# Experts in three fp32r products of split operands, their weights split during attention

## The reference

```
x = x + xattn(layernorm(x), ctx)      # fp8 quantise/dequantise both, one product per batch
hidden = layernorm(x)                 # B=4, S=512, D=512
q, k, v = rmsnorm(hidden) @ w.T       # 16 query heads, 4 key/value heads, hd=128
attn = causal softmax attention with rope and q/k norms
hidden = hidden + attn @ o_w.T
h2 = rmsnorm(hidden) * ffn_norm_w
topv, topi = top_k(softmax(h2 @ gate_w.T), 2)     # E = 8 experts, I = 352
eg, eu = h2 @ wg[e].T, h2 @ wu[e].T
moe = sum over the 2 experts of topw * (silu(eg) * eu) @ wd[e].T
x = x + hidden + moe
```

## Time and profile before

| | |
|---|---|
| time, median of 3 runs | 1544.74 us (1543.94 to 1544.88) |
| the profiled execution | 1543.88 us; its span 1542.1 us |
| PE busy | 1332.3 us, 86% |
| DVE / ACT / POOL busy | 786.9 / 639.6 / 377.8 us |
| PE: up products of the experts (L1515) | 197.2 us |
| PE: down products of the experts (L1532) | 107.0 us |
| mixer, dispatch, experts by their first instructions | 0, 1167.3, 1190 us |

### The profile page before, as it was taken

How to read it: one execution, slowest core, us unless ns; L and a number is a source line. 1 busy time by engine, 2 the same in 40 slices (tenths; PEclk the granted TensorE clock), 3 DMA queues, 4 the chain that set the end, 5 groups by cost and what they waited for, 6 DMA issues and landing times. The chain is left out here.

```text
span 1542.1 us, 20420 instructions
## 1 busy us (share of the span) xinstructions
PE 1332.3 (86%) x6416; PEld 971.2 (63%) x6416; DVE 786.9 (51%) x2389; ACT 639.6 (41%) x2114; POOL 377.8 (25%) x545
## 2 busy tenths in 40 slices
PE   2876989799799989989998999999892799999996
PEld 1564757677576767777676777777671455555653
DVE  7667756556675554577555454544525122222221
ACT  6446644455564545466454544544530111111111
POOL 0322211222222122132212223223101123332331
PEclk9897999999899999999999999999995899999998
DMA  2260324413333241223214122320218833333332
GB/s 89 90 238 21 124 81 166 157 64 129 143 83 121 70 164 56 109 83 83 109 55 161 50 91 82 104 116 4 79 55 270 315 65 69 62 62 69 66 59 40
DMA packets 44505, 156.38 MB, mean 101 GB/s; under 512 B 7089, under 2 KB 7985, under 8 KB 35185
## 3 DMA queue, kind: packets, MB, share of 16 engines
q1 hardware_dynamic: 30624, 129.89, 22.7%
q0 software_dynamic: 10848, 24.71, 9.0%
q10 hardware_dynamic: 2928, 0.49, 0.2%
HBM read 111.00 MB, written 44.06 MB: 101 GB/s over the span
## 5 line engine op out<-in xcount | busy, mean ns | idle before, releaser
L1151 DVE TENSOR_SCALAR_CACHE_REDUCE prob<-bank,nscale 128x128 f32<-128x128 f32 (+3 forms) x256 | 135.3, 546 | 281.7 <-PE bank L614 280.4
L434 POOL TENSOR_TENSOR prob<-prob,rtotal 128x128 f32<-128x128 f32 (+2 forms) x192 | 118.5, 623 | 431.3 <-DVE rtotal L1157 404.7
L846 ACT ACTIVATE pT<-bank 128x512 f32<-128x512 f32 (+3 forms) x256 | 104.1, 432 | 263.3 <-PE bank L622 263.0
L840 ACT ACTIVATE prob<-prob,bias 128x128 f32<-128x128 f32 (+3 forms) x256 | 144.9, 566 | 163.2 <-DVE prob L1151 161.8
L1515 PE MATMUL gu<-we,xT 128*128 x624 | 197.2, 470 | 2.3 <-DVE xT L1578 1.4
L578 PE MATMUL bank<-w_hi,hT_hi 128*128 128x512 f32 x480 | 177.1, 369 | 3.4 <-DVE rot L1116 3.4
L633 PE MATMUL bank<-pT,v 128*128 128x512 f32 (+3 forms) x512 | 176.8, 447 | 2.1 <-ACT pT L846 1.5
L578 PE MATMUL bank<-w_hi,hT_lo 128*128 128x512 f32 x480 | 165.2, 344 | 0.0
L578 PE MATMUL bank<-w_lo,hT_hi 128*128 128x512 f32 x480 | 165.1, 344 | 0.0
L411 POOL TENSOR_TENSOR r<-r,rot 128x640 f32<-128x640 f32 x60 | 96.3, 1604 | 280.1 <-DVE rot L1116 280.1
L1515 PEld LDWEIGHTS gu<-we,xT 128*128 128x128 f32 x624 | 116.6, 192 | 65.7 <-issue 5.0
(11 more groups left out here) (274 smaller groups left out, 2548.3 us busy)
## 6 DMA issues: line engine op xcount, KB each, us to landing
w_hi<-ws_scratch SPq DMA_DIRECT2D x24, 1024.0 KB, 5.0
w_lo<-ws_scratch SPq DMA_DIRECT2D x24, 1024.0 KB, 7.3
we<-in_wexp SPq DMA_DIRECT2D x8, 2176.0 KB, 22.4
stage<-in_wqkvo SPq DMA_DIRECT2D x40, 256.0 KB, 3.0
ws_scratch<-w_hi SPq DMA_DIRECT2D x7, 1024.0 KB, 3.9
ws_scratch<-w_lo SPq DMA_DIRECT2D x7, 1024.0 KB, 7.1
w_hi<-ws_scratch SPq DMA_DIRECT2D x12, 512.0 KB, 5.9
w_lo<-ws_scratch SPq DMA_DIRECT2D x12, 512.0 KB, 6.8
```

Of the source, the lines that this page charges most:

```text
L434: nc.gpsimd.tensor_tensor(p, p, rtotal[:, 4 * h + q:4 * h + q + 1].broadcast_to([P, KEYS[q]]), ALU.mult).then_inc(prob_ready, 1)
L840: nc.scalar.activation(p, p, ACT.Exp, bias=bias[:, 4 * h + q:4 * h + q + 1], scale=-1.0, accum_out=total[:, 4 * h + q:4 * h + q + 1]).then ...
L846: nc.scalar.activation(pT[:, PT_AT[j]:PT_AT[j] + QS[j]], bank[PT + j % 2][:, 0:QS[j]], ACT.Copy).then_inc(pt_copied, 1)
L1151: nc.vector.tensor_scalar(prob[(G * it + h) % (LAG + 1)][:, P_AT[q]:P_AT[q] + KEYS[q]], bank[SC + q % 2][:, 0:KEYS[q]], nscale[it % 2][:, ...
```

## The change

The weights of the experts are split in the mixer. From iteration 5 on, 10 of the 12 places of an iteration get a unit `ew`, 96 in all (12 pieces for each expert: 8 of 352 columns, 4 of 384). A unit is one ACT instruction (hi, scaled by `ffn_norm_w` where it is a gate or up weight), one DVE instruction (lo, written over the raw piece), and on SP one load and two saves. The split weights go to `wx_scratch` in DRAM, 4.4 MB for each expert. In SP's queue the instructions of an iteration are spread over its places in order to stand beside the pieces.

```
@@ mixer: where the units stand, and what they do
+SPLIT_E = [(0, 2), (0, 3), (1, 1), (1, 2), (1, 3), (2, 1), (2, 2), (2, 3), (3, 1), (3, 2)]
+FIRST_E = 5
+    if it >= FIRST_E and slot in SPLIT_E:            # at the end of units()
+        m = (it - FIRST_E) * len(SPLIT_E) + SPLIT_E.index(slot)
+        if m < NPIECE:
+            yield "ew", m
+            def hi_exp(m):                            # ACT
+                act.wait_ge(stage_in[n % RING_W], 16 * (n // RING_W + 1))
+                if m >= RING_E:                       # RING_E = 2
+                    act.wait_ge(ehi_saved[m % RING_E], 16 * (m // RING_E))
+                nc.scalar.activation(o, i, ACT.Copy, scale=wcolf[:, k:k + 1]).then_inc(exp_hi, 1)
+            def lo_exp(m):                            # DVE
+                dve.wait_ge(exp_hi, m + 1)
+                nc.vector.scalar_tensor_tensor(o, i, wcolf[:, k:k + 1], hi, ALU.mult, ALU.subtract).then_inc(exp_lo, 1)
@@ mixer, SP
-                if HKV <= it + 2 < NIT:
-                    load_q(it + 2)
-                    load_kv(it + 2)
+                for h in range(G):
+                    for place in range(1, 4):
+                        for kind, m in units(it, h, place):
+                            if kind == "ew":
+                                save_exp(m)           # waits exp_hi, saves hi; waits exp_lo, saves lo
+                                if m + RING_W < NPIECE:
+                                    load_exp(m + RING_W)   # waits until lo of m is saved
...
+                        if (h, place) == (2, 1) and HKV <= it + 2 < NIT:
+                            load_q(it + 2)
+                        if (h, place) == (2, 2) and HKV <= it + 2 < NIT:
+                            load_kv(it + 2)
@@ mixer, POOL
-            add_hidden(B - 1)
@@ dispatch
-                sp.dma_start(we[:, e * ECOLS:(e + 1) * ECOLS], wexp[e]).then_inc(w_in[e], 16)     # e = 1 to 7
+            load_expert(sp, 0, False)
+            load_expert(sp, 0, True)                  # expert 0 alone, 4 DMAs
+            pool.wait_ge(sources, 1)                  # POOL, when idg is ready
+            for i in range(NG):
+                pool.indirect_dma_start(xg[i][:, :], None, row_dram, ...).then_inc(x_in[i], 16)
+            nc.scalar.activation(iotas[:, :, :], iotab.unsqueeze(2).broadcast_to([P, P, JT]), ACT.Copy).then_inc(spread, 1)
-                pe.wait_ge(onehots, n + 1)
-                last = nc.tensor.matmul(rps[:, :], oh[:, n, :], rhs[:, :, :, n], ...)
+                pe.wait_ge(onehots, 1 if n < NT else 2)
+                last = nc.tensor.matmul(rps[:, :], oh[:, :, n], rhs[:, :, :, n], ...)
-            for n in range(JT):
-                V.tensor_scalar(oh[:, n, :], iotab, lo[:, n:n + 1], None, ALU.is_equal).then_inc(onehots, 1)
+            for c in range(2):                        # two instructions of 128 x 2048 bf16
+                V.tensor_tensor(oh[:, :, some], iotas[:, :, some], lob[:, some]..., ALU.is_equal).then_inc(onehots, 1)
@@ experts, SP: a ring of four experts (RING_WE = 4)
+            for i in range(NG):
+                sp.wait_ge(x_in[i], 16)
+            for e in range(1, RING_WE):
+                load_expert(sp, e, False)             # gate and up, hi and lo: 2 DMAs
+                load_expert(sp, e, True)              # down, hi and lo: 2 DMAs
+            for e in range(RING_WE):
+                landed(e, False)                      # waits, then raises gu_ready
+                landed(e, True)
+            for e in range(RING_WE, E):
+                tiles = sp.value_load(ecum[0:1, e - RING_WE:e - RING_WE + 1], ...)
+                sp.wait_ge(up_done, tiles)
+                load_expert(sp, e, False)
+                landed(e, False)
...
@@ experts, POOL
+            pool.dma_start(out[(B - 1) * S:B * S, :]..., last_acc[:, :, :], accum_op=ALU.add).then_inc(hid_added, 16)
             pool.wait_ge(hid_added, 16 * B)           # before the first tile is added into out
@@ experts, PE (down the same, with 9 matmuls; it waits for dn_ready)
                 for u in range(2):
                     for k in range(KC):
+                        for n, (a, c) in enumerate(SPLITS):
+                            last = nc.tensor.matmul(gu[i % 2][u][:, 0:I], xT[a][i % 2][:, k, :], we[:, bass.ds(at + (c * ECOLS + k * GU + u * I), I)], ...)
@@ experts, ACT per tile, in this order: silu(i), hi_x(i + 1), scale_y(i - 1), hi_hidden(i)
+                nc.scalar.activation(xT[0][i % 2][:, :, :], xtr[:, :]..., ACT.Copy).then_inc(xT_hi, 1)
+                nc.scalar.activation(hT[0][i % 2][:, :, :], htr[:, 0:IP]..., ACT.Copy).then_inc(hT_hi, 1)
@@ experts, DVE per tile: hh(i), lo_x(i + 1), lo of hT(i), slot_weight(i)
-                nc.vector.tensor_tensor(xT[i % 2][:, :, :], xtr[:, :]..., wcolf[:, :]..., ALU.mult).then_inc(xT_ready, 1)
+                nc.vector.tensor_tensor(xT[1][i % 2][:, :, :], xtr[:, :]..., xT[0][i % 2][:, :, :].bitcast(F32), ALU.subtract).then_inc(xT_ready, 1)
```

More of the change, by code:

```diff
@@ L73, in build @@
         logits = ctx.enter_context(nc.sbuf_tensor("logits", [P, NT, E], F32))
-        w_in = [ctx.enter_context(nc.semaphore(f"we_in{e}")) for e in range(E)]
+        wx_dram = nc.dram_tensor("wx_scratch", (E, 2, P, ECOLS), F32, kind="Internal").ap()
         row_dram = nc.dram_tensor("row_scratch", (B * S, ROW), F32, kind="Internal").ap()
@@ L178, in mixer @@
         w = [sb(f"w_{n}", [P, NCH, CH], F32R) for n in ("hi", "lo")]
-        stage = [sb(f"stage{i}", [P, CH]) for i in range(RING_W)]
+        raw = [sb(f"stage{i}", [P, CH], F32R) for i in range(RING_W)]
+        stage = [t[:, :].bitcast(F32) for t in raw]
+        ehi = [sb(f"ehi{i}", [P, IP], F32R) for i in range(RING_E)]
         hT = [sb(f"hT_{n}", [P, KC, S], F32R) for n in ("hi", "lo")]
@@ L1267, with dispatch @@
 NTP = 40
-GU = 2 * I
-ECOLS = KC * GU + IC * D
+RING_WE = 4
 ROUND23 = 1.5 * 2.0 ** 23
 NG = 4
-def dispatch(nc, dispf_d, disph_d, wexp, we, w_in, logits, idg, ids, first, second, eoff, eneed, extra, x2_saved, row_dram, out):
+EARLY = 2
+def dispatch(nc, dispf_d, disph_d, load_expert, logits, idg, ids, first, second, eoff, eneed, ecum, extra, xg, x_in, x2_saved, row_dram, out):
     with ExitStack() as ctx:
@@ L1411, in _ @@
             own.done(V.tensor_copy(hib[:, :], hi[:, :]))
-            own.chain(V.scalar_tensor_tensor(lo[:, :], hi[:, :], -float(P), sl[:, :], ALU.mult, ALU.add))
+            own.chain(V.scalar_tensor_tensor(lob[:, :], hi[:, :], -float(P), sl[:, :], ALU.mult, ALU.add))
             grid = [P, NTP, JT]
@@ L1472, in _, with landed @@
         def _(sp):
-            for e in range(E):
-                sp.wait_ge(w_in[e], 16)
-                sp.sem_inc(w_ready, 1)
+            def landed(e, down):
+                sp.wait_ge((dn_in if down else gu_in)[e % RING_WE], 32 * (e // RING_WE + 1))
+                sp.sem_inc(dn_ready if down else gu_ready, 1)
+            sp.sem_inc(up_done, 1)
+            sp.sem_inc(down_done, 1)
+            for i in range(NG):
[7 more added lines that the diff above has]
+            for e in range(RING_WE, E):
+                tiles = sp.value_load(ecum[0:1, e - RING_WE:e - RING_WE + 1], min_val=1, max_val=NTILE + 1)
+                sp.wait_ge(up_done, tiles)
+                load_expert(sp, e, False)
+                landed(e, False)
+                sp.wait_ge(down_done, tiles)
+                load_expert(sp, e, True)
+                landed(e, True)
         @block.gpsimd
@@ L1531, in down, with expert @@
                 for c in range(IC):
[L1532 to L1533 removed]
+                    for n, (a, b) in enumerate(SPLITS):
+                        last = nc.tensor.matmul(dn[i % 2][:, :], hT[a][i % 2][:, c, :], we[:, bass.ds(at + (b * ECOLS + KC * GU + c * D), D)],
+                                                start=(c == 0 and n == 0), stop=(c == IC - 1 and n == 2))
                 last.then_inc(down_done, 1)
             def offset(i):
[L1537 removed]
+                return pe.value_load(eoff[0:1, i:i + 1], min_val=0, max_val=(RING_WE - 1) * 2 * ECOLS)
+            def expert(i):
+                return pe.value_load(eneed[0:1, i:i + 1], min_val=1, max_val=E)
             transposes(0)
@@ L1547, in _ @@
                 if i:
+                    pe.wait_ge(dn_ready, expert(i - 1))
                     down(i - 1, before)
```

187 lines of the change are left out of this document (129 added, 58 removed).

## The result

The changed kernel takes 1528.19 us in the median of four runs (1517.15 to 1531.57), the kernel before, on the same chip, 1544.34 (1542.49 to 1544.88). The ratio is 0.9882, with an interval from 0.9855 to 0.9909: 1.2% faster, 16 us. The forecast was 1495, 50 us less than before. The direction was right; the time lies above the range.

A forecast was written before the change was run, and what follows sets the result against it. The prediction took PE's matmuls to bound the kernel, each of 39 tiles costing 8.20 us. Its terms, -50.9 for the tiles and +10 for attention the largest, summed to -50.0: 1495 us as a median, range 1477 to 1522.

The forecast's parts named there:

- The tile: Steady tile in the experts: 6.85 us instead of 8.20, with split matmuls 0.1615 us apart, -50.9 us in all.
- rival 1: Experts' matmuls run at their columns' bare pace without a fixed 13 ns, tile 0.43 us shorter: 1479 us, 6%.
- rival 3: In the experts, loading the stationary operand, 0.19 us a bar, bounds split matmuls, tile 7.5 us: 1521 us, 10%.
- rival 4: In the experts, the sequencer needs two register operations per split matmul, tile 9.0 us: 1577 us, 3%.
- point (c): POOL's chain in a tile: each scatter lands 4.8 us after issue, so its period is 5.3 or less against 6.85.
- The barrier: Between mixer and dispatch: without POOL's drain of the accumulating DMA, 7.8 us shrink to about 0.6, -7.2 us.
- Dispatch: Between mixer and experts: shorter one-hots, -1.6 us, and a gather released by its own semaphore, -1.1 us.
- The first tile: Start of the experts: SP issues 12 weight DMAs before signalling expert 0, so the first `up` comes later, +3.7 us.
- Attention: Mixer: ten pieces put 11.2 us more on ACT and DVE per iteration, at 0.094 each, +10 us over 9.6 iterations.
- Rival 2: In the experts, the 1 MB addition lands late, so tiles 4 and on come 10 us late: 1505 us, 12%.
- Rival 5: In attention, the pieces are paid in full, 107 us added: 1592 us, 6%.

The follow-up runs named there:

- experiment 3: The changed kernel with experts 4 to 7 not loaded, their tiles using the weights of experts 0 to 3: 1516.27 us.
- experiment 4: The changed kernel with POOL issuing gather i+4 before it waits for tile i's result: 1520.92 us.
- experiment 12: The kernel of experiment 6 with the second four experts' weights not loaded, the first four's used instead: 1507.58 us.
- experiment 8: The kernel before the change, with only the last addition of the mixer's output moved behind the first four gathers: 1537.40 us.
- experiment 1: The changed kernel with SP signalling expert 0 as landed before it issues the 12 weight DMAs of experts 1 to 3: 1521.55 us.
- experiment 5: The changed kernel with the pieces' ACT and DVE work kept but their transfers removed, the experts loading raw weights: 1527.54 us.
- experiment 13: The kernel of experiment 6 with attention's loads, including `load_o` and `load_x`, issued ahead of the waits for the units: 1509.40 us.
- experiment 6: The changed kernel with the edits of experiment 1 and experiment 4 together: 1518.31 us.
- experiment 7: The kernel of experiment 6 with SP waiting for the addition to land before it issues expert 2's loads: 1519.17 us.
- experiment 9: The kernel of experiment 6 with the split weights' scratch laid out in blocks, so DMA rows are shorter: 1507.02 us.
- experiment 10: The kernel of experiment 6 with attention's weight loads issued ahead of the units of their place, `load_o` and `load_x` not moved: 1510.65 us.

## Why the prediction was wrong

**The tile: right in size, wrong in how long it holds.** 6.88 for 6.85, split matmuls 0.160 apart for 0.1615, none of rivals 1, 3 and 4. What failed is point (c): "one scatter in flight lands 4.8 after its issue and the next needs it, so its period is 5.3 or less against 6.85". The 4.8 is a median from a kernel whose weights had all landed before the steady tiles. With a ring of four experts the reloads run beside tiles 4 to 21, scatters beside them take up to 10.1, and the gather is queued behind. That made -34 of the -50. Experiments 3, 4 and 12 show it from three sides: without reloads, or with the gather ahead, the tiles take 264 us instead of 277 or 280.

**The barrier: right.** -7.3 for -7.2; experiment 8 shows it alone, with 2 us returned by the late addition.

**Dispatch: -0.6 for -2.7.** The one-hots' instructions fell from 5.30 to 2.36 us, as forecast. But "PE then has 16 matmuls left, and five small instructions of DVE beside them" took the matmuls to be short. DVE waited 1.8 us for them (`rps`); the 32 took 4.96 us after, and 5.3 before, at a granted clock of 0.50, the 1.2 GHz level, both times:

```profile
1195.54 4.96 PE L1439 MATMUL rps<-rhs,oh 128*128 128x80 bf16 x32 [7.42 <-DVE oh L1507]
```

DVE had set their pace before, and now PE does. The gather started 1.1 us behind the start of `idg`, before it was 1.6: 0.5 won where 1.1 were forecast.

**The first tile: mis-sized, +13.2 for +3.7.** The mechanism, a signal behind twelve issues, was right; the price of an issue was not. The seven of the earlier trace rows were no measure of the twelfth: it waited 9.2 us. Experiment 1 gives it all back with two moved lines. I had the longest issue of those seven before me, 1394 ns in a row with a median of 444, and passed over it. What makes an issue block stays open.

**Attention: mis-sized, +20.2 for +10.** The rate of 0.094 us a us of work was close or a little low: the elementwise part measures 11 to 14 us over the ten iterations (experiment 5), where the forecast had 10. I put nothing for the transfers. They cost 3 to 7 us more, most of it in iteration 8, through a step that the prediction touched and dismissed: "`load_q`, `load_kv` now stand behind a piece's waits ... nothing is late". It left out `load_o` and `load_x` behind the last head's units, whose lateness hurt nobody who waits for them, but the reduction that started behind them (experiment 13). The 3.5 us between 666.9 and 670.4 go with the clock. These are the windows of iteration 10 with one and the same mixer program, of the changed kernel and of experiment 6 (the third number from the end is the granted clock):

```profile
794.60:864.70 70.10, 63.26 (x331) 48.96 (x329) 42.82 (x143) 36.82 (x120) 16.89 (x28) 0.95 0.48 167
```

```profile
792.70:859.70 67.00, 61.71 (x331) 47.62 (x328) 42.84 (x143) 36.45 (x120) 16.88 (x28) 0.97 0.50 172
```

The same work takes 3.1 us more in the window whose mean granted clock is lower, 0.95 instead of 0.97. What decides between the two stayed open.

**The rivals.** Rival 2 was there, but covered: in the changed kernel the first tile is so late that scatter 0 waits for ACT and not for the addition; without that cover it costs 8 us at tile 4 (experiment 1). The addition landed after 22 us, as the prediction expected; what it had wrong was gather 4 behind it, which it put at 31 us into the block. In experiment 1 that gather was issued after 24 us and took 9.9 to land beside the loads, where the earlier trace rows have 4.3. It is the mistake of point (c) again: a landing read where hardly anything stood beside it. Rival 5's place was right and its size far off.

## What to carry to other kernels

A latency read where the DMA queues are idle doesn't hold once a change puts transfers beside it. Before an operation that is hidden is left at nothing, take the price that its row shows under load, and ask who is queued behind it on its engine. A signal that others wait for goes out before a run of DMA issues, and a gather before the wait for a result. Losses in one pipeline don't add: mending the first brought 5 to 7 us of 13, because the second had stood behind it.

## What the runs showed of the hardware

- An issue of a DMA can block its engine: with long rows the twelfth of twelve loads of 0.77 and 1.4 MB took 8.7 to 9.2 us in nine kernels, where the others took 0.3 to 0.9; in experiment 5 the last three shared it (2.1, 3.8 and 2.9 us). It isn't the twelfth as such: in experiment 7, with a pause behind the fourth, none took over 1.4 us, and with short rows (experiment 9) the sixth took 8.6.
- An indirect scatter of 128 rows lands in 4.8 us by itself and up to 10.6 beside loads of weights in experiment 6, 12.1 in experiment 10; with rows of loads a quarter to a half as long, up to 9.2.
- An accumulating DMA of 1 MB released its waiter 22 us after its issue beside the twelve loads (experiment 1), 34 beside those of seven experts (experiment 8), and 16 beside twelve loads with short rows (experiment 9).
- GpSimd's reduction across partitions starts 5.8 us after the instruction ahead of it with free queues (experiment 5: 5.9), and 9.0 to 9.9 with full ones.
